# First keys and queries by halves of the rows, and products of the identity in gaps of TensorE

## The chip, the cores and the metric

The kernel runs on one core of one Trainium2 chip. The metric is the device time of one execution in microseconds (us), as the median of several runs; lower is better.

## The reference

One transformer block on x (2 batches of 1024 rows, 256 columns) and a context (2 x 154 rows, 192 columns), all in float32:

```
h = layernorm(x);  x = attention(h, h)        @ wo + bo + x     # self, 16 heads of 64, 1024 keys
h = layernorm(x);  x = attention(h, context)  @ wo + bo + x     # cross, 16 heads of 64, 154 keys
h = layernorm(x);  p = h @ w1 + b1;  out = (p[:1024] * gelu(p[1024:])) @ w2 + b2 + x
attention: softmax(q k^T / 8) v, with q = h wq, k = h wk, v = h wv
```

## The kernel before

Every engine has its own order of work, written out by hand. The attention goes in 32 iterations J of one pair of heads each: J = 0 to 15 are self-attention (batch 0, then batch 1), 16 to 31 cross-attention. Operands of the products that need precision are split into a high part (a copy rounded to fp32r, made by ScalarE) and a low part (the rest, made by VectorE for activations and by GpSimd for weights), and each product is three products: high with high, high with low, low with high.

The items of the orders are letters with J and a part. x loads rows, n takes row statistics (VectorE), s takes the root (ScalarE, line 1128), z normalises (VectorE, line 984), t turns the rows by TensorE with the identity (line 866), a applies gain and bias and writes h_hi (ScalarE, lines 1164 and 1166), l writes h_lo (VectorE, line 996). W splits the weights of keys and queries (ScalarE line 1178, then GpSimd line 1344 for the low part), G those of the values (lines 1189 and 1354), O the output weights (lines 1195 and 1359). K and Q make the keys and the queries of one J for all 1024 rows, V the values, each in two turns (line 707): in each turn the two row groups of the array, 64 rows each, work on two halves at a time, the first turn with the one assignment of group to half, the second with the other, so that neither half of the rows is ready before the second turn is. ScalarE copies them out (K line 1207, Q lines 1215 and 1219, V line 1231), VectorE makes the low parts (line 1010). X multiplies queries with keys in one fp32r product (line 792), and VectorE reduces each such block of 128 queries by 512 keys, for two heads, to row maxima (line 1018); there are 16 blocks for each self-attention J, the first 8 for the first half of the queries. C combines them (line 1029), M moves the maxima into a row by DMA (line 626). S makes the scores of 128 keys by 512 queries less the maxima (line 815), ScalarE takes the exponential (line 1244), GpSimd adds the exponentials up for the denominator (A, line 1373), P multiplies them with the values (line 829, plain fp32), E and L split that result (lines 1252 and 1034), D sums the denominators over the partitions (line 840), Y multiplies with the output weights (line 852), and VectorE adds it to x (line 1055). b adds a bias to x on GpSimd (line 1382). The context is turned by c (lines 874, 1171 and 1001). After iteration 31 come the two layers of the feed-forward part (F and H), and their weights are split by i and j.

The orders are strings of such items with a due time each. `stream` expands them for every J and sorts them by due time for each engine, so a number moves an item only when it passes another item of the same engine. Within an engine everything runs in that order, and an instruction that waits for a semaphore holds up all behind it. OPENING is the part ahead of the steady iterations, TURN the change from self- to cross-attention. TensorE has three buffers of two PSUM banks, given out in turn to K, Q, V, X, S, t, c, D and Y, so an item also waits until the former user of its buffer has been read. P uses two banks of its own (PVB = 6 and 7).

Of the kernel before, what the change touches and what calls it, by code (L numbers as in the profile page):

```python
# [32 lines left out]
P = 128  # L33
KD = DM // P
KC, PC = 2, DC // 2
HALF = 512
# [50 lines left out]
V0 = [0]  # L87
# [10 lines left out]

def buffer_of(J, u):

    return (U0[J] + u) % plan_of(J).probs


def user_before(J, u):
# [16 lines left out]
}  # L121
CROSS_ORDER = {
# [5 lines left out]
}  # L128
OPENING = {
# [5 lines left out]
}  # L135
NORM_SELF = {
    "sp": "",
    "pe": "t0.0@13.05 t0.1@13.39 t1.0@25.28 t1.1@35.55",
    "dve": "n0@-21.02 n1@-7.45 z0@-5.92 z1@15.44 l0.0@20.02 l0.1@22.43 l1.0@30.91 l1.1@37.95",
    "act": "s0@-2.86 y0@-0.95 a0.0@11.21 a0.1@14.17 y1@15.47 a1.0@28.58 a1.1@40.21",  # L140
    "pool": "b0@80.42 b1@129.08",
# [159 lines left out]
def release_of(item):  # L301
# [6 lines left out]
    if kind == "K":  # L308
        return "KQ", KQ0[J] + plan_of(J).khalf
# [21 lines left out]
def block_kernel(nc, io, out):  # L331
    with ExitStack() as ctx:
# [351 lines left out]
        def _(pe):  # L684
# [29 lines left out]
            def K(J, turn):  # L714
                plan, item = plan_of(J), ("K", J, 0)
                if turn == 0:
                    wait_buffer(pe, item)
                    pe.wait_ge(s_w_lo, J + 1)
# [720 lines left out]
```

## Time and profile before

| | us |
|---|---|
| median of 3 runs | 1216.65 |
| lowest and highest | 1215.77, 1216.74 |
| the profiled execution: its own time | 1216.77 |
| the profiled execution: its span | 1214.7 |

The span runs from the first to the last instruction. A row of the timeline has the start in us, how long the group lasted, the engine, the line in the code, the operation with its output and inputs, and the number of instructions; in brackets stands how long the engine had been idle, and what ended that. A matmul that follows another starts before the other has drained, so the distance of the starts is what one costs in a chain, not its duration.

### The profile page before, as it was taken

The page shows a single profiled execution, that of the slowest core. Times are in us where ns is not written, and L with a number is a line of the kernel's source. Part 1 is how long each engine was busy: PE and PEld are TensorE (multiplying, and loading weights), DVE is VectorE, ACT ScalarE, POOL GpSimd, SP SyncE. Part 2 cuts the span into 40 slices and gives each one's busy share as a digit, 9 for nine tenths or more (in the row PEclk, how much of TensorE's full clock was granted, in tenths as well). Part 3 has the DMA queues.
Part 4 walks back from the last instruction along what each step waited for, and adds up shares of the span by engine and source line. Part 5 has one row for each costly group of instructions (what it writes and reads, how often), then busy time and mean ns, then how long its engine had stood idle before and what let it go on. Part 6 is the DMA issues. An engine that isn't in the chain of part 4 may idle for free.

```text
span 1214.7 us, 23620 instructions
## 1 busy us (share of the span) xinstructions
PE 1185.2 (98%) x9385; PEld 774.6 (64%) x9385; DVE 768.8 (63%) x1289; ACT 641.8 (53%) x954; POOL 743.1 (61%) x381
## 2 busy tenths in 40 slices
PE   4999999999999999999999999999999999999998
PEld 3655666665666666566656654666666666678887
DVE  4666567566565676675665666368777877774433
ACT  4457544454444447654544444557865586536432
POOL 2296697786786876767977868864545455421000
PEclk9999999999999999999999999999999999999999
DMA  3000000000000000000000000011211110000000
GB/s 112 14 19 23 10 6 23 2 14 19 6 14 19 6 14 19 6 14 10 15 17 6 22 2 13 16 46 25 78 33 45 25 33 18 24 6 18 18 18 18
DMA packets 63539, 25.76 MB, mean 21 GB/s; under 512 B 34551, under 2 KB 61383, under 8 KB 63431
## 3 DMA queue, kind: packets, MB, share of 16 engines
q1 hardware_dynamic: 63375, 24.25, 7.7%
q8 instruction: 75, 1.23, 0.4%
q14 instruction: 33, 0.27, 0.1%
q10 hardware_dynamic: 56, 0.01, 0.0%
HBM read 21.62 MB, written 2.10 MB: 20 GB/s over the span
## 4 chain that ended last, share of the span: by engine, by line
PE 90%; POOL 4%; ACT 2%; DVE 1%; issue 1%; DMA 1%; SPq 0%; ACTq 0%; DVEq 0%; POOLq 0%
PE psum L829 22%; PE psum L815 22%; PE psum L707 15%; PE psum L692 9%; PE psum L852 7%; PE psum L792 6%; POOL acc L1373 4%; PE psum L912 4%; PE psum L840 3%; PE psum L797 2%; PE psum L866 1%; DVE m_part L1018 1%; ACT h_hi L1164 0%; DVE xr L1055 0%; DMA vec_rows<-in_L_xattn_ff_b 0%
## 5 line engine op out<-in xcount | busy, mean ns | idle before, releaser
L1373 POOL TENSOR_TENSOR acc<-acc,probs 128x1024 f32<-128x1024 f32 x192 | 459.1, 2391 | 61.5 <-ACT probs L1244 39.7
L1244 ACT ACTIVATE probs<-psum 128x1024 f32<-128x1024 f32 (+1 forms) x320 | 318.2, 1029 | 283.6 <-PE psum L815 274.5
L1018 DVE TENSOR_REDUCE m_part<-psum 128x2 f32<-128x1024 f32 x256 | 310.0, 1223 | 205.7 <-PE psum L792 205.7
L1373 POOL TENSOR_TENSOR acc<-probs 128x1024 f32<-128x1024 f32 (+1 forms) x64 | 153.3, 2396 | 177.6 <-ACT probs L1244 157.3
L829 PE MATMUL psum<-probs,val 128*64 128x512 f32 x1024 | 244.6, 603 | 0.0
L1055 DVE SCALAR_TENSOR_TENSOR xr<-psum,d_cols,xr 128x256 f32<-128x256 f32 x512 | 207.8, 476 | 35.0 <-PE psum L852 34.6
L829 PEld LDWEIGHTS psum<-probs,val 128*64 128x64 f32 x1024 | 63.4, 136 | 114.4 <-issue 94.1
L815 PE MATMUL psum<-row_max,minus 64*128 64x512 f32 (+1 forms) x640 | 126.0, 389 | 0.0
L815 PE MATMUL psum<-q_hi,k_hi 64*128 64x512 f32 x512 | 101.7, 393 | 0.3 <-DVE m_part L1018 0.3
L815 PE MATMUL psum<-q_hi,k_lo 64*128 64x512 f32 x512 | 101.0, 390 | 0.0
L815 PE MATMUL psum<-q_lo,k_hi 64*128 64x512 f32 x512 | 100.8, 389 | 0.0
L707 PE MATMUL psum<-h_hi,wqk_hi 64*128 64x512 f32 x384 | 79.2, 408 | 3.6 <-DVE h_lo L996 3.6
L707 PE MATMUL psum<-h_lo,wqk_hi 64*128 64x512 f32 x384 | 77.3, 398 | 0.0
L707 PE MATMUL psum<-h_hi,wqk_lo 64*128 64x512 f32 x384 | 76.3, 393 | 0.0
L852 PE MATMUL psum<-wo_hi,o_hi 64*128 64x256 f32 x512 | 73.2, 282 | 2.6 <-DVE xr L1055 2.6
L852 PE MATMUL psum<-wo_lo,o_hi 64*128 64x256 f32 x512 | 72.5, 279 | 0.0
L852 PE MATMUL psum<-wo_hi,o_lo 64*128 64x256 f32 x512 | 72.3, 278 | 0.0
L815 PEld LDWEIGHTS psum<-row_max,minus 64*128 64x128 f32 (+1 forms) x640 | 57.7, 176 | 16.2
L1022 DVE TENSOR_REDUCE cross_m_cols<-psum 128x4 fp32r<-128x616 f32 x64 | 51.0, 796 | 25.8 <-PE psum L797 25.7
L1215 ACT ACTIVATE q_hi<-psum 128x512 fp32r<-128x512 f32 x54 | 32.5, 602 | 58.6 <-PE psum L707 58.6
L792 PE MATMUL psum<-k_hi,cross_q_hi 64*128 64x512 f32 x256 | 55.8, 448 | 4.0 <-DVE q_lo L1010 1.7
L829 PE MATMUL psum<-probs,cross_val 77*64 77x512 f32 x256 | 59.6, 600 | 0.0
(147 smaller groups left out, 2099.3 us busy)
## 6 DMA issues: line engine op xcount, KB each, us to landing
xr<-in_x SPq DMA_DIRECT2D x8, 256.0 KB, 5.3
wqk_raw<-in_L_xattn_sa_wq SPq DMA_DIRECT2D x16, 128.0 KB, 2.5
wqk_raw<-in_L_xattn_sa_wk SPq DMA_DIRECT2D x16, 128.0 KB, 2.4
wv_raw<-in_L_xattn_sa_wv SPq DMA_DIRECT2D x8, 256.0 KB, 2.8
wo_raw<-in_L_xattn_sa_wo SPq DMA_DIRECT2D x16, 128.0 KB, 2.0
d_cols<-d_rows SPq DMA_DIRECT2D x128, 2.0 KB, 2.1
wqk_raw<-in_L_xattn_ca_wq SPq DMA_DIRECT2D x16, 128.0 KB, 2.3
probs<-in_L_xattn_ff_w SPq DMA_DIRECT2D x8, 256.0 KB, 3.3
```

Of the source, the lines that this page charges most:

```text
L692: mm = pe.matmul(out_ap, w, x, start=(i == 0), stop=(i == last))
L707: mm = pe.matmul(psum[:, bank_of(item, n), c:c + width], w, x, start=(turn == 0 and c == 0 and i == 0), stop=(turn == 1 and i == len(steps ...
L792: mm = pe.matmul(bank(bank0 + h), q[r, half * HALF + t * P:half * HALF + (t + 1) * P], k_hi[r, kh * HALF:(kh + 1) * HALF], start=True, sto ...
L815: mm = pe.matmul(psum[0:plan.ks, bank_of(("S", J, u), h), :], w[rows_of(h), ks if i < 3 else slice(0, plan.ks)], x[rows_of(h), qs], start= ...
L829: mm = pe.matmul(psum[d, PVB + half, :], values(J)[0:plan.ks, kt, own], probs[buffer_of(J, u)][0:plan.ks, h, :], start=(kt == 0), stop=(kt ...
L852: mm = pe.matmul(psum[:, bank_of(("Y", J, a), h), t * DM:(t + 1) * DM], o[half][rows_of(h), rows], w[rows_of(h), :], start=(t == 0 and i = ...
L912: mm = pe.matmul(y, x, w, start=(f == 0 and i == 0 and t % 2 == 0), stop=(f == KF - 1 and i == 2), skip_group_check=True)
L1018: dve.tensor_reduce(m_part[:, half, :, t, kh], psum[:, bank0:bank0 + 2, :], AX.X, ALU.max).then_inc(s_x_read, 1)
L1022: dve.tensor_reduce(c_cols[J % 2][:].rearrange("p (h t) -> p h t", h=2)[:, :, 2 * a:2 * a + 2], psum[:, bank0:bank0 + 2, 0:2 * TC].rearran ...
L1055: op = dve.scalar_tensor_tensor(x, psum[:, bank, t * DM:(t + 1) * DM], d_cols[J % 2][:, c0:c0 + 1], x, ALU.mult, ALU.add)
L1244: act.activation(probs[buffer_of(J, u)][0:plan.ks, :, :], psum[0:plan.ks, bank0:bank0 + 2, :], ACT.Exp, scale=SCALE).then_inc(s_exp, 1)
L1373: pool.tensor_tensor(total, last if kt == 1 else total, now, ALU.add).then_inc(s_acc, 1)
```

## The change

Keys and queries of J = 0 are no longer made in two turns over all rows. The new function `first_half` makes one half of the rows in a turn, with all 128 rows of the array at once (6 products of 512 columns for each of K and Q and each half); it waits only for that half of h. ScalarE and VectorE take K half 0, Q half 0, K half 1, Q half 1. The 16 blocks X of J = 0 come in another order: the four blocks of the first key half first, then the four of the second (`block_of`). The X blocks 0 to 3 thus need only the first halves. The counts of the semaphores follow (`split_at`).

TensorE gets 10 products of the identity with itself (128 x 128, plain fp32, into a bank of P that is not in use) before all else, and 3 more behind the turning of the first half of the rows.

All the due times of the order strings are replaced. The order that comes out differs from the one before in these places. ScalarE: W0 goes ahead of the second root s (before it stood behind a of the first half), K0, K1, Q0, Q1 of J = 0 become K0 Q0 G0 K1 Q1, and the first c comes behind them. TensorE: the first turning of the context moves from between Q0 and K1 to behind X block 3; X block 5 goes ahead of V0; P1 goes ahead of X block 15, and X block 0 of J = 1 behind S5. GpSimd: b0 goes behind A15 of J = 0. VectorE: in each self-attention iteration C0 goes ahead of X8, the new X0 ahead of L1, and X13 ahead of K1. ScalarE: in every cross-attention iteration O goes from ahead of E E d to behind them. Beyond these, single items pass one another: bias additions and splits of the feed-forward weights on GpSimd and ScalarE, G and O against M on the DMA queue, some around J = 15 and 16 and the start of the feed-forward part.

```diff
+def split_at(J, kind, a):
+    if J == 0:
+        return 2 * a + (kind == "Q")
+    return KQ0[J] + a + (plan_of(J).khalf if kind == "Q" else 0)
+
+def block_of(J, a):
+    return (a // 8, a % 4, a // 4 % 2) if J == 0 else (a // 8, a // 2 % 4, a % 2)
...
 OPENING = {
-    "pe": "v@-205.00 t0.0+@-150.33 t0.1+@-141.80 t1.0+@-103.87 t1.1+@-85.45 K0+@-83.67 Q0+@-79.47 c0+@-78.00 K1+@-76.82 Q1+@-59.30 X0+@-51.69 ...
+    "pe": "v@-192.399 t0.0+@-191.201 t0.1+@-190.011 t1.0+@-189.093 t1.1+@-186.376 K0+@-102.430 Q0+@-90.072 K1+@-78.815 Q1+@-70.762 X0+@-47.885 ...
-    "act": "s0+@-205.50 s1+@-150.00 a0.0+@-69.91 a0.1+@-45.76 W+@-45.00 a1.0+@-43.56 a1.1+@-32.77 G+@-32.00 c0+@-31.80 K0+@-31.46 K1+@-29.70 ...
+    "act": "s0+@-264.205 W+@-177.278 s1+@-168.747 a0.0+@-78.035 a0.1+@-69.627 a1.0+@-66.432 a1.1+@-54.224 K0+@-54.212 Q0+@-54.201 G+@-53.010 ...
...
+            def first_half(kind, half):
+                item, i = (kind, 0, 0), int(kind == "K")
+                if half == 0:
+                    wait_buffer(pe, item)
+                    pe.wait_ge(s_w_lo, 1)
+                wait_h(pe, 0, (half,))
+                x = slice(half * HALF, (half + 1) * HALF)
+                pairs = []
+                for k in range(KD):
+                    pairs += [(w_hi[:, i, k, :], h_hi[:, k, x]), (w_hi[:, i, k, :], h_lo[:, k, x]), (w_lo[:, i, k, :], h_hi[:, k, x])]
+                products(bank(bank_of(item, half)), pairs).then_inc(s_prep if half else s_half, 1)
...
             def K(J, turn):
+                if J == 0:
+                    return first_half("K", turn)
...
             def X(J, a):
+                if J == 0 and a == 4:
+                    pe.wait_ge(s_hi, split_at(0, "K", 1) + 1)
...
+            def keep_busy(n):
+                for _ in range(n):
+                    pe.matmul(psum[:, PVB, 0:P], ident[:], ident[:], start=True, stop=True)
+
             pe.wait_ge(s_const, 1)
+            keep_busy(10)
...
                 elif kind == "t":
                     turn_h(J, a)
+                    if J == 0 and a == (0, KD - 1):
+                        keep_busy(3)
...
             def K(J, a):           # ScalarE
-                wait_prep(act, ("K", J, 0))
+                if J == 0 and a == 0:
+                    act.wait_ge(s_half, HALF_AT[("K", J, 0)] + 1)
+                else:
+                    wait_prep(act, ("K", J, 0))
```

## Rows read from the trace of the kernel before

**Rows 1.** The page: the chain that ended last, by engine.

```profile
PE 90%; POOL 4%; ACT 2%; DVE 1%; issue 1%; DMA 1%; SPq 0%; ACTq 0%; DVEq 0%; POOLq 0%
```

**Rows 2.** The timeline of the first 17 us: start, us, engine, line, what.

```profile
1.19 0.29 POOL L1324 TENSOR_SCALAR_AFFINE_SELECT ident<-ident 128x128 f32<-128x128 f32 x1 [0.24 <-POOL ident L1322]
...
7.66 1.97 PE L866 MATMUL psum<-ident,z 128*128 128x128 f32 x8
...
9.71 0.30 ACT L1128 ACTIVATE std<-mean_var,eps 128x4 f32<-128x4 f32 x1 [3.95 <-DVE mean_var L972]
...
11.69 1.97 PE L866 MATMUL psum<-ident,acc 128*128 128x128 f32 x8 [2.06 <-DVE acc L984]
...
12.86 0.62 ACT L1178 ACTIVATE wqk_hi<-wqk_raw 128x512 fp32r<-128x512 f32 x1
12.97 0.69 DVE L996 TENSOR_TENSOR h_lo<-psum,h_hi 128x512 fp32r<-128x512 f32 x1 [0.74 <-ACT psum L1166]
...
16.45 0.69 DVE L996 TENSOR_TENSOR h_lo<-psum,h_hi 128x512 fp32r<-128x512 f32 x1 [0.79 <-ACT psum L1166]
```

**Rows 3.** The tile wqk_raw in the first 20 us: DMA issues, first and last start.

```profile
L597 SPq DMA_DIRECT2D wqk_raw<-in_L_xattn_sa_wk x2: 469/469/469, 3.2 to 19.3; - x2
...
DMA to landing us min/median/max: 2.7/3.3/4.5
```

**Rows 4.** The timeline from 17 to 30 us: keys and queries of J = 0, first blocks.

```profile
17.28 0.80 PE L707 MATMUL psum<-h_hi,wqk_hi 64*128 64x512 f32 x2 [3.63 <-DVE h_lo L996]
...
17.85 0.66 PE L707 MATMUL psum<-h_lo,wqk_hi 64*128 64x512 f32 x2
...
22.12 0.43 PE L707 MATMUL psum<-h_hi,wqk_lo 64*128 64x512 f32 x2
...
23.21 0.40 PE L707 MATMUL psum<-h_lo,wqk_hi 64*128 64x512 f32 x2
...
25.55 0.40 PE L707 MATMUL psum<-h_hi,wqk_lo 64*128 64x512 f32 x2
...
27.79 1.22 DVE L1018 TENSOR_REDUCE m_part<-psum 128x2 f32<-128x1024 f32 x1
...
29.52 4.61 DVE L1018 TENSOR_REDUCE m_part<-psum 128x2 f32<-128x1024 f32 x4
```

**Rows 5.** Windows: length, busy time of five engines, granted clock, DMA share, GB/s.

```profile
17.28:22.55 5.27, 5.27 (x25) 4.17 (x26) 0.00 (x0) 0.00 (x0) 1.03 (x1) 1.00 0.32 100
...
28.97:35.84 6.87, 5.85 (x38) 4.52 (x40) 5.68 (x7) 0.00 (x0) 0.94 (x1) 0.50 0.00 0
```

**Rows 6.** TensorE from 31 to 44 us: values V0, V1 and the first score S0.

```profile
31.92 0.58 PE L707 MATMUL psum<-wv_hi,h_hi 64*128 64x256 f32 x2 [0.34 <-DVE m_part L1018]
...
37.73 0.38 PE L707 MATMUL psum<-wv_hi,h_hi 64*128 64x256 f32 x2 [0.27 <-DVE m_part L1018]
...
43.12 0.39 PE L815 MATMUL psum<-q_hi,k_hi 64*128 64x512 f32 x2
```

**Rows 7.** GpSimd and TensorE up to D of J = 0.

```profile
54.65 7.43 POOL L1373 TENSOR_TENSOR acc<-acc,probs 128x1024 f32<-128x1024 f32 x3 [2.78 <-ACT probs L1244]
...
87.47 2.38 POOL L1382 TENSOR_TENSOR xr<-xr,bias 128x1024 f32<-128x1024 f32 x1
...
92.22 1.06 PE L840 MATMUL psum<-acc,ones 128*32 128x512 f32 x8 [1.27 <-POOL acc L1373]
```

**Rows 8.** TensorE's waits from 92 us to the end: us in total, times, longest.

```profile
PE psum L852 <- DVE xr L1055: 2.6, 5, 0.7
```

**Rows 9.** TensorE at 131 us: P, plain fp32 products.

```profile
131.06 3.65 PE L829 MATMUL psum<-probs,val 128*64 128x512 f32 x16
```

**Rows 10.** VectorE in a steady iteration, around L1 and Y of J = 3.

```profile
245.76 0.67 DVE L1034 TENSOR_TENSOR o_lo<-psum,o_hi 128x512 fp32r<-128x512 f32 x1
...
248.58 3.29 DVE L1055 SCALAR_TENSOR_TENSOR xr<-psum,d_cols,xr 128x256 f32<-128x256 f32 x8 [0.41 <-PE psum L852]
252.52 1.23 DVE L1018 TENSOR_REDUCE m_part<-psum 128x2 f32<-128x1024 f32 x1 [0.64 <-PE psum L792]
```

More of the change, by code:

```diff
@@ L137 @@
     "sp": "",
[L138 to L141, printed above, removed]
+    "pe": "t0.0@13.181 t0.1@13.800 t1.0@25.386 t1.1@35.117",
+    "dve": "n0@-21.020 n1@-6.630 z0@-3.658 z1@12.570 l0.0@20.137 l0.1@22.430 l1.0@30.910 l1.1@40.388",
+    "act": "s0@-2.478 y0@0.727 a0.0@11.361 a0.1@13.816 y1@19.609 a1.0@27.950 a1.1@40.337",
+    "pool": "b0@83.025 b1@113.739",
 }
@@ L144 @@
     "sp": "",
-    "pe": "t0.0@19.42 t0.1@24.22 t1.0@38.69 t1.1@42.25",
-    "dve": "n0@-8.76 n1@-5.10 z0@9.91 z1@21.64 l0.0@23.49 l0.1@23.67 l1.0@39.95 l1.1@41.80",
-    "act": "s0@4.60 y0@17.14 a0.0@23.63 a0.1@25.54 y1@37.38 a1.0@42.78 a1.1@43.41",
-    "pool": "b0@8.75 b1@19.26",
+    "pe": "t0.0@19.420 t0.1@24.220 t1.0@38.838 t1.1@41.240",
+    "dve": "n0@-8.760 n1@-4.215 z0@9.482 l0.0@19.682 l0.1@20.898 z1@21.640 l1.0@40.194 l1.1@41.800",
+    "act": "s0@4.600 y0@17.140 a0.0@23.630 a0.1@25.540 y1@37.380 a1.0@42.780 a1.1@43.315",
+    "pool": "b0@8.750 b1@23.615",
 }
@@ L151 @@
     "sp": "",
-    "pe": "t0.0@16.27 t0.1@22.59 t1.0@28.94 t1.1@41.59",
-    "dve": "n0@-2.08 n1@2.01 z0@7.90 z1@7.91 l0.0@18.36 l0.1@24.35 l1.0@37.79 l1.1@47.32",
-    "act": "s0@8.42 y0@13.48 a0.0@17.39 a0.1@21.15 y1@25.13 a1.0@35.31 a1.1@48.83",
-    "pool": "b0@62.31 b1@131.76",
+    "pe": "t0.0@16.318 t0.1@22.390 t1.0@28.503 t1.1@41.649",
+    "dve": "n0@-6.409 n1@2.010 z0@7.900 z1@7.911 l0.0@17.466 l0.1@24.350 l1.0@38.040 l1.1@46.602",
+    "act": "s0@8.677 y0@13.347 a0.0@17.390 a0.1@21.150 y1@25.130 a1.0@33.612 a1.1@48.335",
+    "pool": "b0@62.310 b1@131.767",
 }
 TURN = {
[5 rows of a table removed]
[5 rows of a table added]
 }
 EXTRA = {
-    "sp": "i0@18.32 i1@22.11 i2@22.75 i3@23.49 j0@26.88 j1@34.38",
+    "sp": "i0@18.320 i1@22.110 i2@22.750 i3@23.490 j0@26.880 j1@34.380",
     "pe": "",
     "dve": "",
-    "act": "i0@17.26 i1@20.88 i2@20.89 i3@20.90 j0@31.20 j1@33.22",
-    "pool": "i0@20.50 i1@21.99 i2@25.57 i3@29.52 j0@33.53 j1@36.34",
+    "act": "i0@20.900 i1@21.793 i2@23.803 i3@27.088 j0@30.931 j1@33.296",
+    "pool": "i0@20.500 i1@21.061 i2@26.628 i3@32.037 j0@33.530 j1@36.340",
 }
@@ L308, in release_of @@
     if kind == "K":
-        return "KQ", KQ0[J] + plan_of(J).khalf
+        return "KQ", split_at(J, "K", plan_of(J).khalf - 1) + 1
     if kind == "Q":
@@ L738, in Q @@
             def Q(J, turn):
+                if J == 0:
+                    return first_half("Q", turn)
                 if turn == 0:
@@ L784, in X @@
                     pe.wait_ge(s_turned, 2 * J + 1 + a // 8)
-                elif a == 0:
+                if J == 0 and a == 4:
+                    pe.wait_ge(s_hi, split_at(0, "K", 1) + 1)
+                if plan is CROSS and a == 0:
                     pe.wait_ge(s_turned, 2 * J + 2)
@@ L788, in X @@
                 if plan is SELF:
-                    half, t, kh = a // 8, a // 2 % 4, a % 2
+                    half, t, kh = block_of(J, a)
                     for h in range(2):
@@ L808, in S @@
                         wait_release(pe, ("K", J, 0))
-                    pe.wait_ge(s_kq_lo, KQ0[J] + plan.khalf + half + 1)
+                    pe.wait_ge(s_kq_lo, split_at(J, "Q", half) + 1)
                     pe.wait_ge(s_m[half if plan is SELF else 0], MOVED[J + 1])
@@ L1006, in KQ @@
                 hi, lo = keys(J) if kind == "K" else queries(J)
-                dve.wait_ge(s_hi, KQ0[J] + a + 1 + (plan.khalf if kind == "Q" else 0))
+                dve.wait_ge(s_hi, split_at(J, kind, a) + 1)
                 if kind == "Q":
@@ L1016, in X @@
                 if plan is SELF:
-                    half, t, kh = a // 8, a // 2 % 4, a % 2
+                    half, t, kh = block_of(J, a)
                     dve.tensor_reduce(m_part[:, half, :, t, kh], psum[:, bank0:bank0 + 2, :], AX.X, ALU.max).then_inc(s_x_read, 1)
@@ L1210, in Q @@
                 prep = bank_of(("Q", J, 0), a)
-                wait_prep(act, ("Q", J, 0))
+                if J == 0 and a == 0:
+                    act.wait_ge(s_half, HALF_AT[("Q", J, 0)] + 1)
+                else:
+                    wait_prep(act, ("Q", J, 0))
                 cols = slice(a * HALF, (a + 1) * HALF)
```

40 rows, old and new, of tables (CROSS_ORDER, OPENING, SELF_ORDER, TURN) are left out of this document.

## The prediction, made before the changed kernel ran

> **What bounds the kernel now.** I read the chain that ended last first: 90% of it is TensorE [rows 1]. Behind S0, at 43.12 us [rows 6], the timeline shows TensorE without a gap for whole iterations; the largest class of its waits behind 92 us sums to 2.6 us in 5 waits [rows 8]. So what starts the first score earlier moves the end by as much, as long as no other engine is late, and what is changed on an engine beside TensorE in the steady part is worth nothing. The opening, read second, is another matter: TensorE waits for VectorE, ScalarE and data, and its products are slow. In K and Q of J = 0 a pair of products takes (22.12 - 17.85) / 10 = 0.427 us, later (25.55 - 23.21) / 10 = 0.234 us [rows 4]. That is TensorE at 1.2 and at 2.4 GHz. The column of the granted clock does not show the first slow stretch (it says 1.00 for it), but it does show the second, 28.97 to 35.84 us at 0.50 [rows 5], in which the first values are made.
>
> **The change, step by step.**
>
> *W0 ahead of the second root.* The weights are issued by 3.2 us and take at most 4.5 to land [rows 3], so they are there by 7.7, and their split (0.62) is over before the second root starts at 9.71 [rows 2]. It delays nothing, and its low part on GpSimd, even at the 2.38 of a larger instruction [rows 7], is done by 10.7. It leaves ScalarE's chain of the turned rows, where it cost 0.52 between two gains: the last h_lo ends at 16.6 in place of 16.45 + 0.69 = 17.14 [rows 2]. If the weights landed later, every microsecond past 9.1 would go to the whole opening.
>
> *K and Q by halves.* The first needs only the first two h_lo, which end at 12.97 + 0.69 = 13.66 [rows 2], so it starts 17.28 - 13.66 = 3.6 us earlier [rows 4]. The number of slots stays: 24 pairs of 64-row products before, 24 single 128-row products after, the same columns. Full-height products are not in the opening of the trace; between none dearer and the price of a pair I take the price of a pair. With c out from between them, the 24 take 24 x 0.427 = 10.25 us at the low clock and 24 x 0.234 = 5.6 at the high one. The second K half waits for the last h_lo at 16.6, which costs nothing unless the clock is high from the start (then 0.2).
>
> *When the clock rises.* This decides the size. Before, it rose some 5.2 us after TensorE began K at 17.28 [rows 4], and 3.9 us after it began V at 31.92 (at 35.84) [rows 5, 6]. Now the turnings of the second half start at 11.69, last 1.97 [rows 2] and run straight into K at 13.7. If they count as work, 5.2 us end at 16.9; if only K counts, 3.9 to 5.2 us end at 17.6 to 18.9. If the identity products have already raised it and it stays up, it is high at 13.7. The first maximum block X then starts on VectorE 0.5 us behind the last product (0.5 us for X itself and its drain). With a rise at 16.9: 3.2 / 0.427 = 7.5 products slow, 16.5 fast (3.86), end at 20.75, first reduction at 21.25. With 18.9: 22.15. High throughout: 20.0. Low throughout: 24.5. Before it was 27.79 [rows 4]. I take 21.25, between the ends and by the trace's own 5.2.
>
> The Trainium skill ("TensorE: Matmul & The Clock Gate", Part 1) says that the default is the slow clock and that activity releases it, which the two stretches above agree with; its Part 4 adds that the transpose mode does not count as busy in the same way. By that last rule the turnings give nothing, the rise is at 17.6 to 18.9, and the gain below is up to 0.9 smaller. No row here separates the two, and both values lie in my range.
>
> *From the first reduction to S0.* Reductions in a row are (4.61 - 1.23) / 3 = 1.13 apart [rows 4, 10]. VectorE does X0, the second Q low part (0.6), X1, X2, X3, c (0.4), X4, X5. V0 on TensorE needs the buffer of c and comes behind X5, so it starts 4 x 1.13 + 0.6 + 0.4 + 0.1 = 5.7 us behind the first reduction. From V0 to V1 it took 37.73 - 31.92 = 5.8 us [rows 6] with X5, X6 and X7 between; X5 is now ahead (0.43 at the low clock) and the wait of 0.27 at V1 goes, so 5.1. From V1 to S0 it is 43.12 - 37.73 = 5.4 [rows 6], unchanged in its order. The sum is 16.2 us; before, the same way took 43.12 - 27.79 = 15.3, so 0.9 is given back to the order X5 ahead of V0. S0 comes at 21.25 + 16.2 = 37.45, that is **5.7 us earlier**; 6.9 with the high clock from the start, 4.8 with the rise at 18.9, 2.4 if it never rose before V. Were V fast too, V0 and its second turn would be up to 1.7 us shorter.
>
> *The identity products.* They do not appear in the trace. From below, 128 columns cost what a turning costs, 1.97 / 8 = 0.25 [rows 2]; from above, plain fp32 in P: 16 records in 3.65 us are four units of 512 columns, so 0.91 for 512 and 0.23 for 128 at the high clock, 0.46 at the low one [rows 9]. I take 0.46: ten last 4.6 us from 1.5, when the identity is set, to 6.1, and the turnings start at 7.66. Three last 1.4 from 9.6 to 11.0, and the next turnings wait for VectorE until 11.69 [rows 2]. Both are free; at twice the price the three would delay the turnings by 0.7. Left out of these, nothing covers them. Below nothing they are worth what the clock gives, 0 to 1.2 us as above.
>
> *b0 behind A15 on GpSimd.* From 54.65 GpSimd runs without a gap to D of J = 0, which stood idle for 1.27 us on it; in the middle of that chain sits the bias addition of 2.38 us [rows 7]. Moved behind, the chain is 2.4 us shorter and TensorE is next to be late: **1.3 us saved**. The bias is used by Y ten microseconds later. Worst case, another releaser stands right behind and nothing is saved.
>
> *The other orders.* L1 of each self-attention iteration now stands behind the new X0 on VectorE. In the trace L1 (0.67) ran from 245.76; behind an X of 1.23 that starts about 246.9 it ends at 248.85, so Y starts 0.27 later than 248.58. VectorE then idles 0.64 before the next X at 252.52 [rows 10], which hides it. C0 ahead of X8 moves 0.1 us. O behind E E d in cross-attention moves a short copy into a time when ScalarE waits for TensorE, and its user Y comes microseconds later. The moves on the DMA queue pass single issues of half a microsecond, none of them late before. The feed-forward splits move on engines that idle there; the worst is one GpSimd instruction of about 2.4 us late once. I take all this at 0, with -1 to +1 as its bounds (some of the waits of [rows 8] may go or grow).
>
> **Sum.** The profiled execution took 1216.77 us, of which 1214.7 are the span; the 2.1 around it stay. 1216.77 - 5.7 - 1.3 = **1209.8 us**. The median of the runs is 0.12 lower, which I neglect.
>
> **Rivals.**
>
> *The clock stays low longer.* The products of the identity do nothing and the pauses of K, Q and X keep it low until V: the gain is 2.4 instead of 5.7, with D's 1.3 the time is 1213.1, without it 1214.4. For it: TensorE was slow from 7.66 to 22.5 before, the turnings included. Against: K and Q are now one run of over 5 us, and such a run raised it.
>
> *The clock is high from 13.7 on and partly in V.* Gain 6.9 + up to 1.7 + 1.3: 1206.9 to 1208.6. For it: TensorE works from 7.66 to the end of Q with a pause under 1 us. Against: between 6.1 and 7.66 it is idle, and after Q the X blocks leave it mostly idle again, as before 28.97.
>
> *The gain is given back further on.* All engines start earlier, but a DMA or GpSimd is what bounds J = 0; D waits on. Then 3 to 5 us are left: 1212 to 1213.8. Against: the GpSimd chain is started by an exponential, so it moves with S0.
>
> *Slower.* L1 behind X0, in 15 self-attention iterations, holds o_lo for Y: if the slack of 0.64 - 0.27 = 0.37 us on VectorE is not there, each iteration loses up to 0.67. It decides from 7.0 / 15 = 0.47 us each; at 0.67 it costs 10 and the time is 1219.8. Against it: TensorE waited 5 times in all for VectorE's Y [rows 8], so the buffers have more room than that.
>
> *The first halves bring nothing*, because X, in TensorE's order, still stands behind all of K and Q: then only W's 0.5 us and D's 1.3 would count, 1215.0. But the start of K itself moves by 3.6.
>
> **Chances.** The forecast with a rise between 16 and 19 us 0.57; high clock and more 0.14; low clock 0.11; given back 0.08; nothing 0.05; slower 0.05. A measurement of this kernel tells about 0.2% (2.4 us) from no change. Faster by more than that (below 1214.2): the first three and most of the fourth, 0.87; within it 0.08; slower 0.05. The range for 8 in 10 is 1207.3 to 1213.4.
>
> **What would show it right or wrong.** In the new trace: K at 13.7; spacing of its products falling from 0.43 to 0.23 at about 17; first reduction at 21.3; V0 at 27; S0 at 37.4; identity products over by 6.1 and by 11.0; no wait at D of J = 0; self-attention iterations of the same length as before. The forecast is wrong if K waits for the weights, if S0 has moved by less than 4 us, or if the distance from S0 to the end has changed by more than 2.5 us.

## The result, and the profile after

The changed kernel takes 1209.62 us (median of 5 runs, 1208.40 to 1209.97); the kernel before, on the same chip, 1216.28 (5 runs). The ratio is 0.9943, with an interval of 0.9929 to 0.9956: 6.7 us faster, on a forecast of 1209.8. The profiled execution took 1209.62 us, its span is 1207.5.

The chain that ended last, by engine, on the page of the changed kernel:

```profile
PE 94%; DVE 2%; POOL 1%; ACT 1%; DMA 1%; issue 1%; SPq 0%; DVEq 0%; POOLq 0%; ACTq 0%
```

TensorE was 90% of it [rows 1]; GpSimd's 4% are now 1%. The bound is the same engine, with less ahead of it and beside it. TensorE in the first 21 us of the changed kernel (start, us; L948 is the identity product, L896 a turning, L704 keys and queries of J = 0):

```profile
1.53 4.34 PE L948 MATMUL psum<-ident 128*128 128x128 f32 x20 [1.53 <-POOL ident L1367]
...
7.91 1.12 PE L896 MATMUL psum<-ident,z 128*128 128x128 f32 x8 [0.71 <-DVE z L1021]
8.84 1.48 PE L948 MATMUL psum<-ident 128*128 128x128 f32 x6
11.69 1.97 PE L896 MATMUL psum<-ident,acc 128*128 128x128 f32 x8 [1.37 <-DVE acc L1021]
13.81 0.77 PE L704 MATMUL psum<-h_hi,wqk_hi 128*128 128x512 f32 x1
...
15.23 0.60 PE L704 MATMUL psum<-h_hi,wqk_hi 128*128 128x512 f32 x1
15.65 0.42 PE L704 MATMUL psum<-h_lo,wqk_hi 128*128 128x512 f32 x1
15.91 0.40 PE L704 MATMUL psum<-h_hi,wqk_lo 128*128 128x512 f32 x1
...
20.11 0.39 PE L704 MATMUL psum<-h_hi,wqk_lo 128*128 128x512 f32 x1
```

K starts at 13.81, where it started at 17.28 [rows 4]. Read the distances of the starts: four products are 0.42 to 0.56 apart (low clock), from 15.65 on 0.23 to 0.26 (high clock). The first eight turnings took 1.12 us, the next eight 1.97, so the clock was high, fell and rose again before the end of K. (An identity product is two records: ten are x20 and took 4.34 us, 0.43 each, over by 5.9; three are x6 and took 1.48, over by 10.3.)

The weights, on ScalarE and GpSimd of the changed kernel:

```profile
8.17 0.63 ACT L1215 ACTIVATE wqk_hi<-wqk_raw 128x512 fp32r<-128x512 f32 x1 [1.94 <-DMA wqk_raw<-in_L_xattn_sa_wk]
...
8.96 1.27 POOL L1387 TENSOR_TENSOR wqk_lo<-wqk_raw,wqk_hi 128x512 fp32r<-128x512 f32 x1 [5.04 <-ACT wqk_hi L1215]
```

The split waited for the transfer, and was still over ahead of the second root at 9.71. VectorE and TensorE from there to the first score S0 (L1055 is the reduction of an X block, L719 the values, L845 the scores):

```profile
20.97 1.23 DVE L1055 TENSOR_REDUCE m_part<-psum 128x2 f32<-128x1024 f32 x1 [0.41 <-PE psum L822]
22.12 0.68 DVE L1047 TENSOR_TENSOR q_lo<-psum,q_hi 128x512 fp32r<-128x512 f32 x1
22.71 3.48 DVE L1055 TENSOR_REDUCE m_part<-psum 128x2 f32<-128x1024 f32 x3
26.11 0.47 DVE L1038 TENSOR_TENSOR c_lo<-psum,c_hi 96x308 fp32r<-96x308 f32 x1
26.49 2.35 DVE L1055 TENSOR_REDUCE m_part<-psum 128x2 f32<-128x1024 f32 x2
...
26.84 0.42 PE L719 MATMUL psum<-wv_hi,h_hi 64*128 64x256 f32 x2
...
31.42 0.30 PE L719 MATMUL psum<-wv_hi,h_hi 64*128 64x256 f32 x2
...
36.73 0.39 PE L845 MATMUL psum<-q_hi,k_hi 64*128 64x512 f32 x2
```

The first reduction starts at 20.97 for 27.79 [rows 4], V0 at 26.84 for 31.92, V1 at 31.42 for 37.73, S0 at 36.73 for 43.12 [rows 6]. The clock of the same stretches, in windows of the changed kernel (length, busy time of five engines, granted clock, DMA share, GB/s):

```profile
8.84:15.66 6.82, 5.30 (x21) 4.25 (x20) 4.34 (x14) 5.82 (x9) 1.27 (x1) 0.50 0.41 130
15.66:20.40 4.74, 4.74 (x21) 3.58 (x19) 2.61 (x4) 2.93 (x6) 0.97 (x1) 1.00 0.00 0
22.00:29.25 7.25, 4.68 (x36) 3.71 (x38) 6.84 (x8) 0.94 (x2) 1.26 (x1) 0.77 0.22 68
29.25:37.00 7.75, 7.17 (x96) 6.24 (x96) 6.10 (x7) 3.12 (x6) 0.00 (x0) 0.99 0.17 45
```

The fall between Q and V is still there, now at about 26, but it ends about 2.5 us into V instead of 3.9 us [rows 5, 6]. At the end of J = 0, GpSimd and TensorE of the changed kernel show D (L870) without a wait, b0 (L1425) started ahead of it and not waited for:

```profile
83.61 2.39 POOL L1425 TENSOR_TENSOR xr<-xr,bias 128x1024 f32<-128x1024 f32 x1
...
84.09 1.06 PE L870 MATMUL psum<-acc,ones 128*32 128x512 f32 x8
```

TensorE's waits from 37 us to the end (us in all, times, longest): the class of [rows 8], a little larger, and one wait for GpSimd. It stands at the D of J = 14, at 747.14 us; the kernel before had a wait of 0.3 us at the same D.

```profile
PE psum L882 <- DVE xr L1092: 3.3, 5, 0.9
...
PE psum L870 <- POOL acc L1416: 0.7, 1, 0.7
```

Cut at three marks of TensorE, the two profiled executions differ as follows.

| stretch | before | after | difference |
|---|---|---|---|
| start to S0 | 43.12 | 36.73 | -6.39 |
| S0 to D of J = 0 | 49.10 | 47.36 | -1.74 |
| that D to the D of the last iteration (1067.48, 1060.17) | 975.26 | 976.08 | +0.82 |
| last D to the end of the span | 147.2 | 147.3 | +0.1 |
| span | 1214.7 | 1207.5 | -7.2 |

The third row can be split. From the D of J = 0 to the D of J = 14, all self-attention, the way takes 662.86 us before and 663.05 after; from the D of J = 15 to the last D, all cross-attention, 266.04 and 266.65. So the 0.8 us lost there are 0.2 in self-attention and 0.6 in cross-attention. The repeat of the changed kernel, below, shows the same (662.90 and 266.64).

### The profile page after: what moved, and what is told of

Read it like the earlier page. It is cut to its first block, busy times and chain, and to the rows that moved or that the text cites. A ratio compares the mean times of both kernels' runs of the same rounds, so it can differ in the third digit from the quotient of the medians.

```text
span 1207.5 us, 23622 instructions
## 1 busy us (share of the span) xinstructions
PE 1187.0 (98%) x9387; PEld 779.0 (65%) x9387; DVE 767.8 (64%) x1289; ACT 642.5 (53%) x954; POOL 743.3 (62%) x381
## 4 chain that ended last, share of the span: by engine, by line
PE 94%; DVE 2%; POOL 1%; ACT 1%; DMA 1%; issue 1%; SPq 0%; DVEq 0%; POOLq 0%; ACTq 0%
PE psum L859 24%; PE psum L845 23%; PE psum L719 15%; PE psum L704 9%; PE psum L882 7%; PE psum L822 6%; PE psum L942 4%; PE psum L870 3%; PE psum L827 2%; POOL acc L1416 1%; PE psum L896 1%; DVE xr L1092 0%; DVE m_part L1055 0%; DMA d_cols<-d_rows 0%; DMA xr<-in_x 0%
## 5 line engine op out<-in xcount | busy, mean ns | idle before, releaser
L1055 DVE TENSOR_REDUCE m_part<-psum 128x2 f32<-128x1024 f32 x256 | 310.2, 1223 | 209.5 <-PE psum L822 209.3
L1092 DVE SCALAR_TENSOR_TENSOR xr<-psum,d_cols,xr 128x256 f32<-128x256 f32 x512 | 206.7, 476 | 30.4 <-PE psum L882 30.0
L845 PE MATMUL psum<-row_max,minus 64*128 64x512 f32 (+1 forms) x640 | 126.2, 389 | 0.0
L845 PE MATMUL psum<-q_hi,k_hi 64*128 64x512 f32 x512 | 101.8, 393 | 0.3 <-DVE m_part L1055 0.3
L845 PE MATMUL psum<-q_hi,k_lo 64*128 64x512 f32 x512 | 101.1, 390 | 0.0
L845 PE MATMUL psum<-q_lo,k_hi 64*128 64x512 f32 x512 | 100.9, 390 | 0.0
L719 PE MATMUL psum<-h_hi,wqk_hi 64*128 64x512 f32 x368 | 74.9, 402 | 0.0
L719 PE MATMUL psum<-h_lo,wqk_hi 64*128 64x512 f32 x368 | 73.3, 393 | 0.0
L719 PE MATMUL psum<-h_hi,wqk_lo 64*128 64x512 f32 x368 | 72.6, 389 | 0.0
L845 PEld LDWEIGHTS psum<-row_max,minus 64*128 64x128 f32 (+1 forms) x640 | 57.8, 176 | 16.2
```

What stands on the lines that cost most here:

```text
L719: mm = pe.matmul(psum[:, bank_of(item, n), c:c + width], w, x, start=(turn == 0 and c == 0 and i == 0), stop=(turn == 1 and i == len(steps ...
L845: mm = pe.matmul(psum[0:plan.ks, bank_of(("S", J, u), h), :], w[rows_of(h), ks if i < 3 else slice(0, plan.ks)], x[rows_of(h), qs], start= ...
L1055: dve.tensor_reduce(m_part[:, half, :, t, kh], psum[:, bank0:bank0 + 2, :], AX.X, ALU.max).then_inc(s_x_read, 1)
L1092: op = dve.scalar_tensor_tensor(x, psum[:, bank, t * DM:(t + 1) * DM], d_cols[J % 2][:, c0:c0 + 1], x, ALU.mult, ALU.add)
```

## The experiments

Twelve experiments, in three groups, two of them repeats of a kernel that had run already; those of a group ran on the same chip beside the kernel before. The marks are those of the profiled executions, in us. "Slow" counts the 24 products of K and Q of J = 0 that ran at the low clock: those whose distance to the next is over 0.40. In the kernel before and in b0's, one product has the turning of the context behind it, so its distance says nothing; its own 0.43 and 0.41 us, where a product at the low clock takes 0.66, show that it had the high one. For the kernel before, its profile is the one shown ahead.

| kernel | group | K starts | slow | first reduction | S0 | span | median (lowest to highest), n | ratio to before, interval |
|---|---|---|---|---|---|---|---|---|
| before | | 17.28 | 11 | 27.79 | 43.12 | 1214.7 | 1216.33 / 1216.83 / 1216.57 in groups 1 / 2 / 3 | |
| changed | | 13.81 | 4 | 20.97 | 36.73 | 1207.5 | 1209.62 (1208.40-1209.97), 5 | 0.9943, 0.9929-0.9956 |
| changed, again | 3 | 13.48 | 7 | 21.25 | 37.24 | 1206.8 | 1208.93 (1208.07-1209.79), 5 | 0.9937, 0.9925-0.9950 |
| no identity products | 1 | 13.65 | 9 | 21.75 | 37.91 | 1208.3 | 1209.94 (1209.64-1210.64), 5 | 0.9948, 0.9934-0.9961 |
| the ten alone | 1 | 13.46 | 7 | 21.36 | 37.40 | 1207.7 | 1209.83 (1208.62-1211.03), 5 | 0.9947, 0.9934-0.9959 |
| the three alone | 1 | 13.80 | 0 | 20.21 | 36.60 | 1206.8 | 1209.39 (1208.88-1210.19), 5 | 0.9943, 0.9931-0.9956 |
| twenty (13, 1, 6) | 1 | 13.49 | 0 | 19.91 | 35.82 | 1206.2 | 1208.67 (1208.01-1211.04), 5 | 0.9941, 0.9929-0.9953 |
| twenty, again | 3 | 14.35 | 0 | 20.75 | 36.56 | 1206.6 | 1208.63 (1207.78-1209.59), 5 | 0.9936, 0.9923-0.9950 |
| before + b0 behind A15 | 2 | 16.86 | 10 | 27.13 | 42.47 | 1213.1 | 1215.72 (1214.39-1216.34), 11 | 0.9990, 0.9981-0.9999 |
| new opening, old orders behind | 2 | 13.49 | 13 | 22.41 | 38.99 | 1209.3 | 1209.83 (1209.22-1211.36), 5 | 0.9944, 0.9931-0.9956 |
| W0 back behind a | 2 | 14.55 | 7 | 22.33 | 38.31 | 1208.6 | 1211.68 (1210.72-1212.97), 5 | 0.9958, 0.9946-0.9971 |
| K and Q in two turns again | 2 | 16.89 | 9 | 27.34 | 43.98 | 1213.7 | 1215.63 (1215.24-1216.62), 11 | 0.9992, 0.9983-1.0000 |
| V0 ahead of X5 | 3 | 13.72 | 0 | 20.15 | 36.53 | 1206.3 | 1210.05 (1208.37-1211.15), 5 | 0.9945, 0.9933-0.9958 |
| twenty and fill up to V | 3 | 13.65 | 7 | 21.50 | 36.06 | 1206.4 | 1207.81 (1206.27-1208.27), 5 | 0.9927, 0.9914-0.9939 |

Subtract S0 from the span: with b0 behind A15, that is in every row but the first, 1169.6 to 1170.8 is left (before: 1171.6). The ends differ because the first score does. One profile against another therefore shows the clock of that execution as much as the edit; the medians decide, and they carry a microsecond of scatter.

Part of that scatter can be seen in the clock of the single runs. The five runs of the changed kernel in group 3 had mean granted clocks of 0.998, 0.997, 0.996, 0.996 and 0.995 and took 1208.07, 1208.56, 1208.93, 1208.96 and 1209.79 us. It is not the whole of it: the five runs of its first measurement all had 0.996 and spread over 1.6 us.

**What the identity products are worth.**

```diff
             pe.wait_ge(s_const, 1)
-            keep_busy(10)
...
                     turn_h(J, a)
-                    if J == 0 and a == (0, KD - 1):
-                        keep_busy(3)
```

> The changed kernel without the 13 products of the identity; all else as changed. Theory A (they raise the clock sooner): without them the rise comes 3.9 to 5.2 us after K starts at 13.8, as in the two stretches of the kernel before, so at 17.7 to 19.0 in place of 15.7; about five to eight products of K and Q more are slow (0.43 in place of 0.23), the first reduction comes 1.0 to 1.5 us later than 20.97 and the time is 1210.6 to 1211.1. The turnings of the first half take 1.97 us in place of 1.12. Rival B (the clock rises by K itself and by the turnings just ahead of it, the identity products do nothing): rise at 15.7 again, time 1209.6 within 0.3.

TensorE of the kernel without them:

```profile
7.75 1.97 PE L896 MATMUL psum<-ident,z 128*128 128x128 f32 x8 [0.25 <-DVE z L1018]
11.53 1.97 PE L896 MATMUL psum<-ident,acc 128*128 128x128 f32 x8 [1.81 <-DVE acc L1018]
13.65 0.76 PE L704 MATMUL psum<-h_hi,wqk_hi 128*128 128x512 f32 x1 [0.15 <-DVE h_lo L1030]
...
17.20 0.58 PE L704 MATMUL psum<-h_hi,wqk_lo 128*128 128x512 f32 x1
17.61 0.39 PE L704 MATMUL psum<-h_hi,wqk_hi 128*128 128x512 f32 x1
```

The turnings are slow, nine products are slow, and the clock rises at 17.6. The granted clock says 1.00 for all of it, as it did for K of the kernel before [rows 5]. The gain is nearly all there without the products. The rise is as late as theory A says, but the first reduction is only 0.8 us later than in the changed kernel and the median 0.3 us, less than either number of theory A and not told apart from rival B.

The ten alone leave the second `keep_busy` out:

> Only the 10 products at the start, without the 3 behind the turning of the first half. Theory A has the 10 raise the clock early (the turnings at 7.9 are fast) but the clock falls again at 8.8 before K; what makes it rise soon in K is the stretch just ahead of K, to which the 3 belong: then the rise is late, 17.7 to 19.0, time 1210.6 to 1211.1, as without any. Rival B: 1209.6. Rival C (the 10 are what matters): 1209.6 here, and 1210.6 to 1211.1 with only the 3.

The first turnings took 1.09 us, the second 1.97, and seven products were slow: the ten raised the clock, and it did not last. The three alone:

> Only the 3 products behind the turning of the first half, without the 10 at the start. The turnings of the first half are slow again (1.97 us), which nobody waits for. If the 3 are what brings the early rise in K: rise near 15.7, time 1209.6 within 0.3. If the 10 are: rise at 17.7 to 19.0, time 1210.6 to 1211.1. If neither does anything: 1209.6.

TensorE of the kernel with the three alone:

```profile
9.66 1.49 PE L948 MATMUL psum<-ident 128*128 128x128 f32 x6
11.68 1.80 PE L896 MATMUL psum<-ident,acc 128*128 128x128 f32 x8 [0.53 <-DVE acc L1020]
13.80 0.47 PE L704 MATMUL psum<-h_hi,wqk_hi 128*128 128x512 f32 x1 [0.32 <-DVE h_lo L1032]
```

The first turnings, ahead of these lines, took 1.97 us. The second took 1.80 where they take 1.97 at the low clock, so the clock rose near their end, and no product of K was slow. More of them, 13 ahead of all else, 1 behind the turning of the vectors, 6 behind the first half:

```diff
-            keep_busy(10)
+            keep_busy(13)
...
+                    keep_busy(1)
...
-                        keep_busy(3)
+                        keep_busy(6)
```

> More products of the identity in the gaps: 13 at the start (they end at 7.2, some 0.2 us behind the landing of the vectors), 1 behind the turning of the vectors, 6 behind the turning of the first half (they end at 10.9 to 11.5, before the next turnings at 11.7). If filled gaps keep the clock up from 5.9 on, K and Q run fast throughout: the second K half then waits for h_lo until 16.6, the first reduction comes at 20.0 in place of 20.97, and the time is 1208.7. If the clock falls at the same place all the same, nothing changes: 1209.6. If the products hold up the turnings, up to 0.5 us worse: 1210.1.

TensorE of this kernel:

```profile
7.67 1.04 PE L896 MATMUL psum<-ident,z 128*128 128x128 f32 x8
8.54 1.50 PE L948 MATMUL psum<-ident 128*128 128x128 f32 x12
11.71 1.26 PE L896 MATMUL psum<-ident,acc 128*128 128x128 f32 x8 [1.66 <-DVE acc L1022]
13.49 0.47 PE L704 MATMUL psum<-h_hi,wqk_hi 128*128 128x512 f32 x1 [0.53 <-DVE h_lo L1034]
13.80 0.40 PE L704 MATMUL psum<-h_lo,wqk_hi 128*128 128x512 f32 x1
```

Six of them cost 1.50 us at the high clock, the products are 0.31 and then 0.23 to 0.24 apart from the first on, and the first reduction is 1.8 us ahead of the kernel without any (19.91 against 21.75). The medians of the four (none, ten, three, twenty) are 1209.94, 1209.83, 1209.39 and 1208.67, and the intervals of all four overlap, so they do not tell the four apart. To see whether the profiles repeat, two of the kernels ran again:

> The changed kernel again, unaltered, to be compared with the next three and for another look at the clock. By the theory that the clock rises and falls at its own moments, with a phase that differs from one execution to the next, the first reduction comes anywhere from 20.0 to 22.5 us (20.97 before, 22.41 with the same opening in the kernel with the old steady orders), and the time is 1209 to 1211. By the rival, that it follows from the instructions alone, the first reduction is at 20.97 within 0.2 again.

> The kernel with 13, 1 and 6 products of the identity again, beside the changed one on the same chip. If filled gaps make the high clock in K likelier, K is fast from its start again, the first reduction is at 20 and the time 0.5 to 1.0 us below that of the changed kernel. If the first look was luck, K starts slow in this profile and the two times are alike within 0.3.

The changed kernel, the same program, had seven slow products in place of four. Twenty products again had none, but the medians of the two are 0.3 us apart, which the expectation gave to luck; and in a third profile with the same twenty ("twenty and fill up to V", below) the clock was high at the start of K, fell at about 14.0 us, and seven products were slow. So twenty do not secure the high clock either. Four runs in which the opening up to K is the same code ("changed", "changed, again", "new opening, old orders behind", "V0 ahead of X5") had 4, 7, 13 and 0 slow products. In all four the clock was high at some time between the ten and K: in three during the first turnings, in the fourth during the ten themselves, which took 3.91 us there, and in three (the fourth among them) during the second turnings (1.25, 1.26 and 1.32 us). What differs is when it falls: in "changed, again" it fell at 13.3 us, 0.2 ahead of K, in "new opening, old orders behind" at 12.4. One profile of one of these kernels says little about it.

**b0 alone**, on the kernel before:

```diff
-    "pool": "f@-200.00 W+@-186.00 G+@-41.34 W++@-41.16 b0+@84.77 b1+@97.72",
+    "pool": "f@-200.00 W+@-186.00 G+@-41.34 W++@-41.16 b0+@95.73 b1+@97.72",
```

> The kernel before with one item moved: the first bias addition on GpSimd (b0, 2.38 us) behind A15 of J = 0. Theory A: GpSimd's chain was what D of J = 0 waited for, so its wait of 1.27 us goes, S0 stays at 43.1, and the time is 1216.3 - 1.3 = 1215.0 (down to 1214.6, since from S0 to D the changed kernel takes 47.4 in place of 49.1). Rival: the wait is taken over by another releaser, or given back by the bias coming later: 1216.3 within 0.3.

D of this kernel, on TensorE:

```profile
90.19 1.06 PE L840 MATMUL psum<-acc,ones 128*32 128x512 f32 x8
```

It waits for nothing; from S0 (42.47) it is 47.72 us away, 1.38 less than before. The median is 1.1 us lower, with an interval of 0.1 to 2.3 us. The term of 1.3 stands by the trace, and the median agrees.

**The orders behind the opening.** The strings from J = 0's successors on are those of the kernel before; only the opening (with b0) is new.

> The changed kernel with all due times but those of the opening put back to the ones before (the bias addition b0 stays behind A15, being in the opening). Theory A: the orders of the steady iterations are worth nothing: 1209.6 within 0.5. The traces leave room for both signs: from S0 to D of J = 0 the changed kernel is 0.4 us shorter than the wait explains (then 1210.0 here), and in cross-attention it is 0.5 longer (then 1209.1 here). Rival: they matter by more than 1 us.

The way from S0 to D is 47.82 us, from D to the last D 975.50, where the changed kernel has 47.36 and 976.08. The new orders win 0.5 in the one and lose 0.6 in the other, and the medians are 0.9944 and 0.9943 of the kernel before. Together they are worth nothing that can be measured. The 0.6 us lie in cross-attention: from the D of J = 15 to the last, this kernel takes 266.08 us, the kernel before 266.04, and the changed one 266.65 and 266.64 in its two profiles. (That its profile had 13 slow products is the clock's doing; its own other runs are 1209.2 to 1210.0.)

**W0's place.**

```diff
-    "act": "s0+@-264.205 W+@-177.278 s1+@-168.747 a0.0+@-78.035 a0.1+@-69.627 a1.0+@-66.432 ...
+    "act": "s0+@-264.205 s1+@-168.747 a0.0+@-78.035 a0.1+@-69.627 W+@-69.000 a1.0+@-66.432 ...
```

> The changed kernel with the split of the first weights (W0) back at its old place on ScalarE, behind the first half of the gains. Theory A: the low part of the weights is then ready only at about 14.8, so K starts 1.0 us later than 13.8, and the second half of h comes 0.5 us later; with part of it hidden by a clock that rises at its own time, the first reduction comes 0.5 to 1.0 us later and the time is 1210.1 to 1210.6. Rival: the place of W0 costs nothing, since K's first products are slow anyway: 1209.6.

GpSimd and TensorE of this kernel:

```profile
13.19 1.26 POOL L1387 TENSOR_TENSOR wqk_lo<-wqk_raw,wqk_hi 128x512 fp32r<-128x512 f32 x1 [9.28 <-ACT wqk_hi L1215]
...
14.55 0.77 PE L704 MATMUL psum<-h_hi,wqk_hi 128*128 128x512 f32 x1 [2.05 <-POOL wqk_lo L1387]
```

K waits for the weights' low part. In the kernel before, with the same place of W0, it was ready at 14.9 us, ahead of the last h_lo, which K waited for. The median is 1.85 above that of the new opening on the same chip (1211.68 against 1209.83), but the two intervals overlap, and four of the five runs had a mean granted clock of 0.993 or 0.994, where four of the other kernel had 0.996 or 0.997. Profiles with equally many slow products show the edit by itself: seven here and seven in "changed, again", first reduction 22.33 against 21.25 and S0 38.31 against 37.24, so 1.1 us. The rest of the 1.85 is not shown to be W0's. Halves need W0 early; this I had priced at 0.5.

**The halves themselves.** K and Q of J = 0 by two turns over all rows again; the early W0, the identity products and every order stay.

```diff
             def K(J, turn):
-                if J == 0:
-                    return first_half("K", turn)
...
-                if J == 0 and a == 0:
-                    act.wait_ge(s_half, HALF_AT[("K", J, 0)] + 1)
-                else:
-                    wait_prep(act, ("K", J, 0))
+                wait_prep(act, ("K", J, 0))
```

> The changed kernel with K and Q of J = 0 made in two turns over all rows as before; the identity products, the early W0, the order of the X blocks and all orders stay as changed. Theory A: K can start only at 16.7 (last h_lo) in place of 13.8, and the first queries are ready only behind the last product, so that ScalarE's copies stand between them and X: first reduction at about 26 in place of 20.97, time 1214.5 to 1215.5. Rival B: only the start of K counts, 2.9 us: 1212.5. Rival C: the halves are worth little beside the clock and the bias: below 1211.

TensorE, ScalarE and VectorE of this kernel:

```profile
16.89 0.79 PE L719 MATMUL psum<-h_hi,wqk_hi 64*128 64x512 f32 x2 [3.11 <-DVE h_lo L1029]
...
23.20 0.60 ACT L1240 ACTIVATE k_hi<-psum 128x512 fp32r<-128x512 f32 x1 [7.19 <-PE psum L719]
...
27.34 1.22 DVE L1051 TENSOR_REDUCE m_part<-psum 128x2 f32<-128x1024 f32 x1
```

K starts 3.1 us later, ScalarE stands idle for 7.2 us until the first k_hi, and the first reduction is back at 27.3. It starts 3.2 us behind the last product of K and Q (24.15), where it is 0.9 in the changed kernel: both parts of theory A are there, and rival B has only the first. The time is that of b0 alone (0.9992 and 0.9990). Against the new opening on the same chip the halves are worth 1215.63 - 1209.83 = **5.8 us**, given the early W0 (the two kernels differ in the orders behind the opening too; by the ratios of this kernel and the changed one, 0.9992 and 0.9943, it is 6.0). The early W0 and the identity products without the halves bring nothing that can be seen.

**V0 ahead of X5** as before, to test the 0.9 us that the prediction gave back to this order:

```diff
-    ... c0+@-41.761 X4+@-30.686 X5+@-30.577 V0+@-27.713 X6+@-6.942 ...
+    ... c0+@-41.761 X4+@-30.686 V0+@-30.600 X5+@-30.577 X6+@-6.942 ...
```

> The changed kernel with V0 ahead of X block 5 on TensorE, as before the change. By the sentence of the prediction that 0.9 us are given back to the order X5 ahead of V0, this is 0.9 faster than the changed kernel. By the trace of the changed kernel it is 0.2 to 0.6 slower: V0 waits for the low part of the context, which ends only at 26.5, so it would start 0.3 us sooner at best, and X5 would come 2.5 us later, with VectorE idle for 1.8.

VectorE of this kernel:

```profile
25.66 1.21 DVE L1055 TENSOR_REDUCE m_part<-psum 128x2 f32<-128x1024 f32 x1
28.70 3.49 DVE L1055 TENSOR_REDUCE m_part<-psum 128x2 f32<-128x1024 f32 x3 [1.83 <-PE psum L822]
```

V0 starts 5.27 us behind the first reduction instead of 5.87, and VectorE then waits 1.83 us for X5, which stands behind V0's products. S0 comes 16.4 us behind the first reduction; with X5 ahead it was 15.8 to 16.6 in the nine profiles that have it, halves, and no filling behind Q. The median is 1.1 above the changed kernel on the same chip, intervals overlapping. Nothing is won by going back; that it costs something is not shown.

**Filling up to V.** The 20 of above, and 4, 1 and 2 identity products behind X1, X3 and X4 and 2 behind the first c, so that TensorE works on where it waits for VectorE:

> As the one before, and also 4, 1 and 2 products of the identity behind X blocks 1, 3 and 4 and 2 behind the first turning of the context, so that TensorE is not idle between Q and V. If the clock then stays high until V0, the first turn of V0 takes 1.4 in place of 2.5 us and X6 is in time for VectorE: S0 comes 1.0 to 1.5 us sooner than without them (34.5), time 0.8 to 1.5 below the kernel without these nine. If the clock falls all the same, or TensorE is held up by them: equal, or up to 0.5 slower.

TensorE of this kernel:

```profile
25.64 0.50 PE L822 MATMUL psum<-k_hi,cross_q_hi 64*128 64x512 f32 x2
26.07 0.71 PE L948 MATMUL psum<-ident 128*128 128x128 f32 x4
26.78 0.50 PE L822 MATMUL psum<-k_hi,cross_q_hi 64*128 64x512 f32 x2
27.16 0.38 PE L719 MATMUL psum<-wv_hi,h_hi 64*128 64x256 f32 x2
27.38 0.28 PE L719 MATMUL psum<-wv_lo,h_hi 64*128 64x256 f32 x2
27.49 0.28 PE L719 MATMUL psum<-wv_hi,h_lo 64*128 64x256 f32 x2
```

Its windows from 20 us on (length, busy time of five engines, granted clock, DMA share, GB/s):

```profile
20.00:23.80 3.80, 3.20 (x21) 2.14 (x19) 3.15 (x5) 1.45 (x3) 1.24 (x1) 1.00 0.35 100
23.80:27.20 3.40, 3.22 (x24) 2.01 (x20) 3.40 (x5) 1.05 (x2) 0.72 (x1) 1.00 0.17 47
27.20:30.60 3.40, 3.40 (x54) 3.19 (x54) 3.30 (x3) 0.00 (x0) 0.56 (x1) 1.00 0.00 0
```

The clock no longer falls between Q and V, and this is the only profile in which it does not: in each of the thirteen others the granted clock goes to 0.50 between 22.1 and 29.0 us and is still there when V starts. Here V's products are 0.12 apart where they were 0.21 in the changed kernel, and S0 is 14.56 us behind the first reduction, not 15.8 to 16.6. The filling costs the X blocks nothing (VectorE runs from 22.64 to 30.4 without a pause). K itself had seven slow products in this profile, so the two effects have not been seen together. Its median, 1207.81, is the lowest of all: 0.8 below the twenty without the filling, the low end of the expectation, and 1.1 below the changed kernel on the same chip. The intervals overlap (0.9914 to 0.9939, 0.9923 to 0.9950, 0.9925 to 0.9950), so the gain is likely and not proven. It is the version I would keep.

## Why the prediction was right

The sum was 1209.8 for a profiled execution of 1209.62. That the two are so close is partly luck: S0 came 0.7 us sooner than forecast (36.73 for 37.45), and from S0 to the end 0.8 us were won in place of 1.3. The mechanism was right: the halves bring the first maxima forward, S0 follows, and the end follows S0. Step by step:

- *W0.* The weights landed at about 8.15 us, 4.9 behind the last issue, not by 7.7 as [rows 3] bounded it. The margin up to 9.71 absorbed it. What I missed is its price with halves: not 0.5 but 1.1 us by profiles of like clock and 1.9 by the medians, since a late low part would now be last ahead of K.
- *K and Q by halves.* Full-height products cost what a pair costs (0.43 and 0.23), K at 13.8 for 13.7: the lower case "none dearer" held. This step is the gain, 5.8 us by experiment. The 5.7 of the forecast is another quantity, S0 in all, with W0 and the clock in it; that came out at 6.4.
- *The clock.* The rise came at 15.7, not 16.9, in the profiled execution, so four products were slow instead of 7.5, and the first reduction started at 20.97 (21.25 forecast). In the other runs of the same opening it was up before K, or came at 16.6 and 19.2 after a fall just ahead of K. So 15.7 lies outside the case "between 16 and 19" to which I gave 0.57. The 5.2 us that I took from the trace were read too long: the product at 22.12 takes 0.43 us, where products at the low clock take 0.66 [rows 4], so the rise was at about 22.1, 4.8 behind the start of K. And over all profiles with slow products in K the rise comes 1.8 to 5.7 us behind its start. My central value was the middle of what it does, and the prediction was wrong to treat it as one number that a trace can fix.
- *From the first reduction to S0.* V0 5.87 behind it (5.7, though its terms add up to 5.6), V0 to V1 4.58 (5.1, as the clock rose sooner), V1 to S0 5.31 (5.4): 15.76 in all for 16.2. Before, it was 15.3, so 0.4 is given back, not 0.9; and the blame was misplaced. Of it 0.4 is c_lo, which now stands between the reductions (26.11), where it used to run while VectorE was idle; the order X5 ahead of V0 costs nothing that its reversal would return.
- *The identity products.* Free as forecast (0.43 each, over by 5.9 and 10.3). Their worth of 0 to 1.2 us is the range that the medians leave: 1209.94 without, 1209.62 and 1208.93 with (0.6 and 1.3 us apart by the ratios to the kernel before on the same chip). Five runs each do not resolve it.
- *b0.* 1.3 forecast, 1.38 in the trace and 1.1 (0.1 to 2.3) in the median of that edit alone.
- *The other orders.* 0 with -1 to +1: -0.4 up to D of J = 0 and +0.8 behind, within 0.1 of nothing in the medians. L1 behind X0 costs no iteration what the rival needed (7.0 / 15 = 0.47 us): from the D of J = 0 to that of J = 14 the changed kernel loses 0.2 us in all, less than its wait at the last of these grew (0.4). The 0.6 us lost in cross-attention go with the new orders, since the old ones do not show them; which of the moves it is, no run separates.

The forecast and the rivals by the runs: "the clock stays low" until V happened in none, the nearest being the rise at 19.2; "high from 13.7 on" happened once in the four runs of the changed opening, and in three of the six with another number of identity products or none, so it deserved more than the 0.14 I gave; "the first halves bring nothing" and "given back further on" are out, as the span follows S0 one to one, within 1.2 us.

On the turnings as work for the clock, which decided between a rise at 16.9 and one at 17.6 to 18.9, the runs do not settle the question. Without identity products the rise came at 17.6, 4.0 us behind the start of K, though turnings ran straight into it; in the kernel of two turns it came 4.0 us behind the start of K as well, with TensorE idle for 3.1 us ahead. By these two the turnings brought nothing. The three alone speak against it: there the clock rose at about 13.2, ahead of K, and nothing but turnings, the three identity products (1.49 us) and one small turning of the vectors had run before. The Trainium skill ("TensorE: Matmul & The Clock Gate", Part 4) says that a transpose does not count as busy in the same way; the first two traces would agree with that, the third does not bear it out. The same section adds that the high clock is not engaged for transposes. As a statement on their speed that does not hold here, since eight of them took 1.12 us with the clock up and 1.97 with it down.

Open are the exact worth of the ten and the three, and why the same program finds the clock high at K in one execution and low in another. Neither was found in the profiles: the stretches ahead of K in "changed, again" and "V0 ahead of X5" hold the same instructions, and all but the three identity products (8.39 and 9.51) start within 0.4 us of the same times.

## What to carry to other kernels

Where every engine waits for the first product of a chain, cut the first unit of work to what its first consumer needs (here half of the rows, then the maxima of that half), and check which other input then comes last: the weights' low part would have taken a fifth to a third of the gain. Look at the operation in the middle of a chain that TensorE waits on and that nobody needs soon (b0); moving it behind was a one-number edit for 1.1 us. Where the clock matters, compare medians of several runs and not two profiles, and try filling all gaps up to the work that matters rather than a few of them: here only the kernel that did so kept the high clock into V, in one profile, and its lead in the medians is inside the overlap of the intervals.

## What the hardware did that I had not expected

- The clock at a given instruction is not a property of the program: 0, 4, 7 and 13 of 24 products slow in four kernels with the same opening, which moves S0 by up to 2.5 us and the time with it.
- The clock can fall again just ahead of the work that it was raised for: at 12.4, 13.3 and 14.4 us in three profiles, 0.2 to 1.1 us ahead of K.
- The granted clock reads 1.00 until its first recorded change: the slow K of the kernel without identity products stands under 1.00, told only by the 0.43 us between its starts.
- A plain fp32 product of 128 x 128 shows as two records and costs 0.43 us at the low clock and some 0.2 at the high one (x12 in 1.50, the drain of the last included).
- The first weights, issued by 3.2 us and behind the rows of x, took 4.9 us to land in the changed kernel and 4.5 in its repeat, where a maximum of 4.5 stood in the trace of before [rows 3].
